# The down product of a gated LoRA MLP as seven block multiplications of a 2x2 split

## The reference, cut to what matters

```python
# x: 64 sequences of 64 tokens, 512 wide (4096 tokens); H = 512, I = 2048, 8 adapters of rank 16, fp32
def lora_linear(x, W, A, B, idx):            # idx: the adapter of each sequence
    return x @ W + (x @ A[idx]) @ B[idx]
gate = lora_linear(x, Wg, Ag, Bg, idx)
up   = lora_linear(x, Wu, Au, Bu, idx)
h    = silu(gate) * up                       # 4096 x 2048
x    = x + lora_linear(h, Wd, Ad, Bd, idx)   # the down product
x    = x + w1[idx].T @ x                     # per sequence, a 64x64 matrix over the 64 tokens
```

## Time and profile before

| | |
|---|---|
| median of three runs | 1229.32 us (1228.62 to 1229.39) |
| the profiled execution's own time | 1230.07 us, its span 1228.4 us |
| granted TensorE clock, mean | 0.991 |
| busy share TensorE, VectorE, ScalarE, GpSimd | 97%, 62%, 42%, 10% |
| moved by DMA | 217 MB, 177 GB/s over the span |
| stage one | up to 799.7 us |
| down stage and tail | 799.7 to 1228.4 us |

### The profile page before, as it was taken

The page is one execution under the profiler, slowest core; times in us unless marked ns, Lnnn a source line. Parts: engine busy times, 40 slices in busy tenths (PEclk is TensorE's granted clock), DMA queues, the critical chain, the costliest instruction groups (busy, mean ns, idle before and its releaser), DMA issues.

```text
span 1228.4 us, 22972 instructions
## 1 busy us (share of the span) xinstructions
PE 1197.1 (97%) x7104; PEld 1072.3 (87%) x7104; DVE 758.4 (62%) x1338; ACT 517.1 (42%) x983; POOL 119.7 (10%) x207
## 2 busy tenths in 40 slices
PE   4899999999999999999999999999999999999997
PEld 3678888888888888888888888899999999999997
DVE  6666667766676766667766677654554544554543
ACT  4544444544444544444544454443333333333332
POOL 5223100001100000100000000011111111111110
PEclk8899999999999999999999999999999999999999
DMA  5597664776566578557466777666545555545530
GB/s 191 165 279 234 207 177 128 196 226 193 157 187 172 144 199 244 152 161 197 122 193 195 215 212 214 187 198 197 156 144 161 164 173 153 157 144 167 172 106 36
DMA packets 113629, 217.15 MB, mean 177 GB/s; under 512 B 26338, under 2 KB 68450, under 8 KB 113506
## 3 DMA queue, kind: packets, MB, share of 16 engines
q1 hardware_dynamic: 104096, 190.41, 53.6%
q0 software_dynamic: 8544, 23.60, 5.8%
q10 hardware_dynamic: 866, 1.66, 0.4%
HBM read 169.43 MB, written 46.14 MB: 175 GB/s over the span
## 4 chain that ended last, share of the span: by engine, by line
PE 46%; SPq 2%; issue 1%; DVE 1%; DMA 1%; ACT 1%; ACTq 0%
PE ps L1138 6%; PE ps L1142 5%; PE ps L1146 5%; PE ps L1145 5%; PE ps L1140 5%; PE ps L1147 4%; PE ps L991 4%; PE ps L992 4%; PE ps L993 4%; PE ps L1003 2%; SPq L270 1%; PE ps L1173 1%; PE ps L1174 1%; PE ps L1175 1%; SPq L165 1%
## 5 line engine op out<-in xcount | busy, mean ns | idle before, releaser
L991 PE MATMUL ps<-xo_hi,w_hi 128*128 128x512 f32 x896 | 357.1, 398 | 11.2 <-DVE w_lo L684 10.5
L992 PE MATMUL ps<-xo_lo,w_hi 128*128 128x512 f32 x896 | 352.9, 394 | 0.0
L993 PE MATMUL ps<-xo_hi,w_lo 128*128 128x512 f32 x896 | 350.3, 391 | 0.0
L991 PEld LDWEIGHTS ps<-xo_hi,w_hi 128*128 128x128 f32 x896 | 170.1, 190 | 41.2 <-DVE w_lo L684 10.5
L993 PEld LDWEIGHTS ps<-xo_hi,w_lo 128*128 128x128 f32 x896 | 169.1, 189 | 37.5
L992 PEld LDWEIGHTS ps<-xo_lo,w_hi 128*128 128x128 f32 x896 | 170.2, 190 | 26.3
L1003 PEld LDWEIGHTS ps<-t_st,bq 128*128 128x128 f32 x1024 | 157.5, 191 | 28.8 <-POOL bq L345 6.6
L684 DVE TENSOR_TENSOR hl<-h_raw,hh 128x1024 fp32r<-128x1024 f32 x64 | 78.4, 1225 | 154.6 <-ACT hh L417 154.6
L1003 PE MATMUL ps<-t_st,bq 128*128 128x256 f32 x1024 | 164.4, 284 | 7.7 <-POOL bq L345 5.8
L1138 PE MATMUL ps<-wd_hl,hh 128*128 128x320 f32 x512 | 160.2, 313 | 0.0
L684 DVE TENSOR_TENSOR w_lo<-wsum,w_hi 128x512 fp32r<-128x512 f32 x116 | 82.2, 708 | 123.7 <-ACT w_hi L417 123.7
(11 more groups left out here) (76 smaller groups left out, 1546.0 us busy)
## 6 DMA issues: line engine op xcount, KB each, us to landing
bq<-b_dram SPq DMA_DIRECT2D x992, 64.0 KB, 2.2
h_dram<-h_f SPq DMA_DIRECT2D x64, 512.0 KB, 3.6
h_raw<-h_dram SPq DMA_DIRECT2D x64, 512.0 KB, 4.1
raw<-packed SPq DMA_DIRECT2D x58, 512.0 KB, 5.3
ad_raw<-a_d SPq DMA_DIRECT2D x64, 128.0 KB, 2.8
xs<-x POOLq DMA_DIRECT2D x16, 512.0 KB, 5.2
y_out_dram<-ys POOLq DMA_DIRECT2D x30, 256.0 KB, 3.5
xst<-xg SPq DMA_DIRECT2D x14, 512.0 KB, 6.4
```

The source lines that it names most:

```text
L991: pe.matmul(bank, st[0], mv[0], start=start and kk == 0, stop=False, skip_group_check=True)
L992: pe.matmul(bank, st[0], mv[1], start=False, stop=False, skip_group_check=True)
L993: m = pe.matmul(bank, st[1], mv[0], start=False, stop=kk == 1, skip_group_check=True)
```

## The change

The down product of a pair is cut into 2x2 blocks: h into tokens (tile 0, tile 1) by chunks (even, odd), the weights into chunks (even, odd) by the two halves of the output. Seven products of 8 chunks each stand in for eight. The sums of h that four of them need (S1 to S4) are made by VectorE in stage one from two neighbouring steps and stored beside the plain blocks, so `h_dram` holds seven operands per pair; the sums of the weights (T1, T2, T3, N4) are made in the last group of stage one, two of them going through DRAM to their places. To make a pair's tiles neighbours in one group, the order of tokens in the pairs changes (`seq_of`, and the layout of `x` and the output). The partial sums are no longer joined in PSUM alone: eight additions of 128x256 per pair into `xs` (`add_p1` to `make_x22`). Only four products carry adapter columns, of which one carries a difference (`ad_diff`). B rows of the down adapter and the mix matrices are split once for all adapters into DRAM tables (`bd_dram`, `w1_dram`) and gathered split.

```diff
-PAIRS, PT = 16, 256
-BAT = 4
+PAIRS, KC = 16, CH // 2
+PRODUCTS = 7
+H11, HS1, H22, HS2, H12, HS3, HS4 = range(PRODUCTS)
+WD11, WDT1, WDN4, WDT2, WD21, WDT3, WD22 = range(PRODUCTS)
+AD_SLOTS = (WD11, WDT1, WDN4, WD21)
+AD_SLOT_AFTER = ((4, 5, 6, 6), (1, 2, 4, 5))
...
-        h_dram = nc.dram_tensor("h_dram", (PAIRS, P, CH, PT), F32, kind="Internal").ap()
+        h_dram = nc.dram_tensor("h_dram", (PAIRS, PRODUCTS, P, KC, P), F32, kind="Internal").ap()
...
 # SyncE, stage one, step s
                 if fresh(s + 2):
                     load_w(s + 2)
+                if s % 2:
+                    store_even(s - 1)
+                else:
+                    store_odd(s - 1)
                 if s >= 2 and s // 2 + 1 < GROUPS * PIECES:
                     at = s % 2 * (SLOTS // 2)
                     gather_b(s // 2 + 1, at, at + SLOTS // 2)
-                store_h(s - 1)
+                if s % 2:
+                    store_s3(s // 2)
+                    if s >= 3:
+                        store_s4(s // 2 - 1)
+                else:
+                    store_s12(s // 2 - 1)
+                if 5 <= s % CH < 13 and s // CH + 1 < GROUPS:
+                    for b in range(2 * (s % CH - 5), 2 * (s % CH - 4)):
+                        b += (s // CH + 1) * SLOTS
+                        slot_numbers[b] = number(sp, b)
                 if s % CH == 2 and s // CH + 1 < GROUPS:
                     load_x(s // CH + 1)
...
 # SyncE, change-over and down stage
+            load_n4()
+            load_h(1)
+            load_wd21()
+            load_h(2)
+            load_h(3)
+            load_wdt3()
+            load_h(4)
+            load_bd(0)
+            load_h(5)
+            load_wd22()
+            load_h(6)
+            store_odd(STEPS - 1)
+            load_ad(1)
+            for n in range(3, PAIRS * PRODUCTS):
+                p, i = divmod(n, PRODUCTS)
+                if n + 4 < PAIRS * PRODUCTS:
                     load_h(n + 4)
...
+                if i == 3 and p + 1 < PAIRS:
+                    load_bd(p + 1)
+                if i == 5 and p + 2 < PAIRS:
+                    load_ad(p + 2)
...
 # VectorE: sums of h, of two steps 2n and 2n+1
+                dve.tensor_tensor(hs3[:, :], h_f[0][:, 0:HALF], h_f[0][:, HALF:GT], ALU.subtract).then_inc(hs3_done, 1)
+                dve.tensor_tensor(hs1[:, :], h_f[0][:, HALF:GT], h_f[1][:, HALF:GT], ALU.add).then_inc(hs1_done, 1)
+                dve.tensor_tensor(hs2[:, :], hs1[:, :], h_f[0][:, 0:HALF], ALU.subtract).then_inc(hs2_done, 1)
+                dve.tensor_tensor(hs2[:, :], h_f[1][:, 0:HALF], hs2[:, :], ALU.subtract).then_inc(hs4_done, 1)
...
 # VectorE, stage one, step s
                     w_lo_raw(s + 1)
+                if s % 2 == 0:
+                    make_s1(s // 2 - 1)
+                    make_s2(s // 2 - 1)
+                elif not last:
+                    make_s3(s // 2)
+                    if s >= 3:
+                        make_s4(s // 2 - 1)
+                if more:
                     w_lo_sum(s + 1, 0)
                     w_lo_sum(s + 1, 1)
...
 # VectorE, last step and down stage (products n = 7 p + i)
             make_h2(s - 1)
             make_h1(s - 1)
+            make_s3(s // 2)
+            make_s4(s // 2 - 1)
             h_lo(0)
+            make_ad_diff(0)
+            wd_lo(WDT2)
             make_c11(s)
             ad_lo(0, 0)
+            ad_lo(0, 1)
             make_u3(s)
             make_c22(s)
+            wd_lo(WDN4)
+            ad_lo(0, 2)
             make_c12(s)
+            for n in range(PAIRS * PRODUCTS):
+                if i == 0 and p:
+                    make_x12(p - 1)
+                    make_x22(p - 1)
+                    x1_split_lo(p - 1, 0)
+                if i == 1:
+                    td_first(p, 0)
+                    add_p1(p)
+                if i == 2:
+                    td_first(p, 1)
+                    add_p5(p)
+                if i == 4:
+                    add_u2(p)
+                if i == 6:
+                    if p == 0:
+                        add_p4(p)
+                    add_u3(p)
+                if n == 0:
+                    h_lo(1)
+                    make_h2(STEPS - 1)
+                    make_h1(STEPS - 1)
+                if n + 2 < PAIRS * PRODUCTS:
                     h_lo(n + 2)
+                if i == 3:
+                    td_add(p, 1)
+                    td_mask(p, 1)
+                    td_lo(p, 1)
+                if i == 5:
+                    td_add(p, 0)
+                    td_mask(p, 0)
+                    td_lo(p, 0)
                     if p:
+                        add_p4(p)
+                if n == 1:
+                    wd_lo(WD21)
+                    ad_lo(0, 3)
+                if n == 3:
+                    wd_lo(WDT3)
+                if n == 4:
+                    wd_lo(WD22)
+                if n == 6:
+                    make_s1(STEPS // 2 - 1)
+                    make_s2(STEPS // 2 - 1)
+                if n == 9:
+                    make_s4(STEPS // 2 - 1)
+                if i == 0 and p:
+                    x1_split_lo(p - 1, 1)
...
+                if i == 6:
+                    make_x11(p)
...
 # TensorE, one chunk of a product
+                width = HD + TR if i in AD_SLOTS else HD
+                h_hi, h_lo = hh[n % 3][:, k, :], hl[n % 3][:, k, :]
+                pe.matmul(bank[:, 0:width], h_hi, w[:, 0:width], start=start and k == 0, stop=False, skip_group_check=True)
+                pe.matmul(bank[:, 0:width], h_hi, w[:, width:2 * width], start=False, stop=False, skip_group_check=True)
+                return pe.matmul(bank[:, 0:width], h_lo, w[:, 0:width], start=False, stop=False, skip_group_check=True)
...
+                pe.wait_ge(h_lo_done, n + 1)
+                if p == 0:
+                    pe.wait_ge(wd_lo_done, WD_ORDER.index(i) + 1)
+                if i in AD_SLOTS:
+                    pe.wait_ge(ad_lo_done, 4 * p + AD_SLOTS.index(i) + 1)
+                if i == HS2:
+                    pe.wait_ge(p1_added, p + 1)
+                if i == HS3:
+                    pe.wait_ge(u2_added, p + 1)
+                if i == HS4:
+                    pe.wait_ge(p5_added, p + 1)
+                for k in range(KC):
+                    m = down(n, k, i in (H11, HS1, H22, H12))
+                    if k == KC - 1:
+                        m.then_inc(product_done, 1)
+                    at = i, k
+                    if p and at == ((HS2, 5) if p == 1 else (HS1, 1)):
+                        mix_tile(p - 1, 0)
+                    if p and at == ((HS2, 6) if p == 1 else (HS1, 5)):
+                        mix_tile(p - 1, 1)
+                    if at == ((H12, 2) if p else (HS3, 5)):
+                        turn(p, 1)
+                    if at == ((HS3, 1) if p else (HS4, 1)):
+                        lora_down(p, 1, 0, rd).then_inc(lora_21_done, 1)
+                    if at == (HS4, 2 if p else 3):
+                        turn(p, 0)
+                    if at == (HS4, 6):
+                        lora_down(p, 0, 0, rb).then_inc(lora_11_done, 1)
+                        lora_down(p, 0, 1, rc)
+                        pe.wait_ge(u3_added, p + 1)
+                        lora_down(p, 1, 1, ra).then_inc(lora_22_done, 1)
```

More of the change, by code:

```diff
@@ L219, in gather_b @@
                 g, k = divmod(n, PIECES)
-                if k == first == 0:
-                    for b in range(SLOTS):
-                        slot_numbers[b] = number(sp, g * SLOTS + b)
                 sp.wait_ge(b_stored, 16 * (k if g == 0 else PIECES))
@@ new lines, in ad_hi @@
+                for w in wd_hl[op]:
+                    n = w.shape[1]
+                    if op == WDN4:
+                        src = ad_diff[:, k:k + n, :].rearrange("p k (s r) -> p k s r", s=2)
+                    else:
+                        src = ad_raw[:, 2 * j:2 * j + 2, e, k:k + n, :].rearrange("p s k r -> p k s r")
+                    m = hi(w[:, :, AHI:AHI + TR].rearrange("p k (s r) -> p k s r", s=2), src)
+                    k += n
+                m.then_inc(ad_hi_done, 1)
@@ new lines, in _ @@
+            for n in range(PAIRS * PRODUCTS):
+                p, i = divmod(n, PRODUCTS)
+                more = p + 1 < PAIRS
+                if i == 0 and p:
+                    x1_split_hi(p - 1, 0)
+                if n == 0:
+                    h_hi(1)
+                if n + 2 < PAIRS * PRODUCTS:
+                    h_hi(n + 2)
+                if i == 6:
+                    td_turn(p, 0)
+                if i == 3:
+                    td_hi(p, 1)
+                if i == 5:
+                    td_hi(p, 0)
+                if n == 1:
+                    wd_hi(WD21)
+                    ad_hi(0, 3)
+                if n == 3:
+                    wd_hi(WDT3)
+                if n == 4:
+                    wd_hi(WD22)
+                if n == 3:
+                    clear_mix()
+                if i == 0 and p:
```

(48 more changed lines are left out.)

920 lines of the change are left out of this document (535 added, 385 removed).

## The result

The changed kernel takes 1248.12 us (1241.71 to 1249.90), the kernel before 1229.32: a ratio of 1.0145, 95% interval 1.0108 to 1.0181. It is 19 us slower by the medians; 1202 was predicted, with a range of 1180 to 1226.

What follows compares the result with a forecast made beforehand. The prediction took both stages to be bound by how fast TensorE starts matmuls. From 1230.07 us profiled, -48 - 1.5 + 10 + 7 + 2 + 3 = -27.5 gave 1202.5, a median of 1202, range 1180 to 1226.

Steps and rivals of the forecast that it cites:

- Term 1: Down stage to its last matmul: 168 product matmuls per pair in place of 192 on TensorE, -48 us.
- term 2: Down-stage pairs: TensorE waits 0 to 0.5 us in each of 15 pairs, +2 us (bounds 0 and 8).
- rival B: Down stage: h loads queue and land in 8 us, each pair waits 1 to 1.5 us; about 1221 us, chance 0.13.
- Term 6: Tail after the last down matmul: 8.1 us in place of 9.5, -1.5 us (bounds -3 and +1).
- Term 3: Stage one: SyncE's extra stores and waits for h1 delay gathers behind x loads, +10 us (bounds 0 and 30).
- rival C: Stage one: SyncE becomes the bound, 2.3 us late in each of 31 pairs of steps; 1263 us, chance 0.08.
- Term 4: Change-over from stage one to down stage: TensorE waits for VectorE and ScalarE splits, +7 us (bounds 2 and 15).
- Term 5: Clock: drops to half speed after stalls of 2 to 4 us in terms 3 and 4, +3 us (bounds 0 and 15).

## Why the prediction was wrong

**What bounds the kernel** before was read rightly: TensorE in both stages.

**Term 1 (-48) and term 2 (+2): right.** 23.6 us per pair for 23.3 + 0.13; over 15 pairs term 2 is +4 to +5, inside its bounds of 0 and 8. VectorE and ScalarE hide seven splits per pair, and rival B fell: an h load lands in 5.5 us, under the 6 that I had named as the limit.

```profile
h_raw<-h_dram SPq DMA_DIRECT2D x112, 512.0 KB, 5.5
```

**Term 6 (-1.5): about right.** 1238.45 to 1247.0 is 8.55 us for 8.1.

**Term 3 (+10): the step that failed.** Stage one is 44 us longer, 14 over the upper bound, its share of the clock drops included. I added 2.2 us of stores per two steps to SyncE, found that 1.2 us of its spare time were left, and priced only single places. Measured, its own work rose from 10.1 to 12.3 us per step, 4.4 per two steps, where 3.8 were free in the 24.0 of two steps: nothing was left. Of the missing 2.2 us, 1.9 are found from start to start of SyncE's issues:
- A number read costs 0.63 us in place of 0.27 behind a full store of sums, and from start to start 0.94 to 1.00 us in place of 0.6. That is 0.7 us in each of eight steps of a group, so 0.7 per two steps; I had counted the reads as they were.
- Other issues stretched a little: gather to gather 0.54 us on average in place of 0.52, 0.7 per two steps; the first gather stands 0.84 us behind a plain store, where it stood 0.76 behind a weight load, 0.2; the five more stores take 2.5 and not 2.2.

Beside this, and no part of own work, the stores of the plain blocks moved ahead of the gathers and wait for `h1`. I had counted 0.9 us for that: with the sums on ScalarE's queue the last gather still comes at 10.1 us, with the gathers ahead and x spread at 7.7, before at 6.6.

The shape of the loss is what a sum of places cannot give: as long as the last gather is issued before about 12 us, lateness is free; beyond it TensorE waits, and often runs at half clock behind the wait. From 10.1 to 11.6 us of own work stage one grows by 13 us, from 11.6 to 12.0 by 27 to 32. But own work is a mean over steps, and single late steps hide in it. The kernel without number reads (11.2 us) ends stage one 11 us later than the one with small stores (11.6): its gathers are late in the few steps behind the loads of x and of down weights, where it keeps the full stores. That reading is from its trace alone and was not tried.

This was **rival C**, which I gave 0.08: "decides from 0.50 us per gather, and from 0.53 on the change is slower than before". The mean over the gathers was already 0.52 in the kernel before, and the two numbers I had set against each other (7.53 and 9.10 for 16) average to it; I took the lower for my sum. The sign that I had named for C, a first down matmul after 825 us, came: 843.65. The Trainium skill (Perfetto Trace Analysis, What "DMA-bound" means) names this case, an issuing engine's track that is solid DMA slices; by that rule the trace of the changed kernel agrees, with 23 us of waits in 690. The Trainium skill (DMA: Bandwidth & Descriptors, Rules for kernel authors) says that spreading transfers over the issuing engines gives no bandwidth and only saves sequencer time. The run with the sums on ScalarE's queue agrees with its second half: the same bytes, 32 us less.

**Term 4 (+7): too small.** The change-over costs the rest of the down stage, 394.8 - 371 - 4 = 20 us: 11.2 of waits (850 to 907 us) and 17 us at half clock, 8.5 lost. I found the places that I had walked (h(1) 3.0 us for 1.9, T3's split and `u2`'s add 3.0 for 2.1); missing was the wait of 3.95 us for the h of the eleventh product, and most of the half clock. The load of that h stands on SyncE behind the stores of the last sums, for which SyncE waits 7.3 us, and behind the adapter loads:

```profile
877.87 1.10 SPq L245 DMA_DIRECT2D h_dram<-hs  x2
880.12 3.65 SPq L371 DMA_DIRECT2D ad_raw<-a_d  x4
883.87 1.32 SPq L362 DMA_DIRECT2D h_raw<-h_dram  x3
```

**Term 5 (+3): the size failed.** The longest wait is 4.2 us, about as counted, but there are ten drops: 13.6 + 8.5 = 22 us lost, over the upper bound of 15. Before, a wait of 1.9 us had left the clock at 2.4 GHz, and I leaned on that.

The sum of what was measured: 34 (stage one over term 3) + 13 (term 4, clock included) + 2 (term 2) + 0.5 (tail) - 3 (term 5, now in the others) = 46.5, and the profiled run is 46.2 over 1202.5.

## What to carry to other kernels

Before adding transfers to a queue, add up that engine's own work per round (its time less its semaphore waits) and compare it with the round of the bound engine; take the mean of its issue distances, not the smallest, and look at the fullest step beside the mean. Ask how long after the bound engine's last step the last urgent transfer is issued, put urgent loads ahead of stores that wait for results, and put the stores on another engine's queue. A wait that another engine shows (45 us on VectorE here) does not say what it costs until it is taken away.

## What the runs showed of the hardware that was not expected

- A register read of a number on SyncE takes 0.27 us behind a gather of 64 KB, 0.30 behind a store of 32 KB, and 0.63 behind one of 256 KB in 512-byte rows.
- The stores of the sums made SyncE's issues dearer, not the transfers later: the last gather landed 2.3 us after its issue in the changed kernel and 2.5 in the one before, while the DMA engines moved 212 GB/s in place of 185. The median over all gathers is 2.4 us for 2.2.
- The granted clock fell to 0.50, in spans of 3.4 or 6.8 us, ten times between 100 and 900 us in the changed kernel, each time during or right behind a TensorE wait of 2.0 to 4.2 us. Not every such wait had one: behind that of 3.4 us which ended at 89.6 us the clock stayed at 1.00.
